# A fused attention and mixture-of-experts kernel: the weight roundings follow attention's older order, the last of them come behind it, and the last two rows go ahead of the first expert tile

## The reference

```python
def _L0_xattn_ref(hidden_states, memory_tokens, memory_mask):
    scores = einsum('bsd,bmd->bsm', hidden_states, memory_tokens) / sqrt(D)
    scores = where(memory_mask[:, None, :], scores, -1e30)
    readout = einsum('bsm,bmd->bsd', softmax(scores), memory_tokens)
    return where(any(memory_mask), readout, 0)

def _L0_ffn_ref(x, w_router, w_gate, w_up, w_down):   # 8 experts, 192 inner, top 2
    probs = softmax(xt @ w_router.T)
    top_v, top_i = top_k(probs, 2); top_v = top_v / sum(top_v)
    comb = zeros((T, 8)).at[arange(T)[:, None], top_i].add(top_v)
    g = einsum('th,eih->tei', xt, w_gate); u = einsum('th,eih->tei', xt, w_up)
    return einsum('tei,ehi,te->th', silu(g) * u, w_down, comb)

x = x + tanh(g_xattn[0]) * _L0_xattn_ref(_layernorm(x), ctx_2048, mask_BxS2_bk0)
x = x + tanh(g_ffn[0]) * _L0_ffn_ref(_layernorm(x), w_router, w_gate, w_up, w_down)
```

## Time and profile before

| | us |
|---|---|
| median of 3 runs (lowest, highest) | 289.17 (288.73, 289.31) |
| the profiled execution's own time | 288.54 |
| its span | 286.7 |
| PE busy / DVE busy | 250.5 / 176.5 |
| ACT busy / POOL busy | 149.9 / 165.7 |

### The profile page before, as it was taken

One profiled execution on the slowest core, in us unless ns is written; L12 is line 12 of the kernel. 1 busy time (PEld: TensorE's weight loads), 2 busy tenths in 40 slices (PEclk: granted clock), 3 DMA queues, 4 the chain that ended last, 5 costly groups with the idle time before them and its releaser, 6 DMA issues.

```text
span 286.7 us, 5375 instructions
## 1 busy us (share of the span) xinstructions
PE 250.5 (87%) x1464; PEld 210.7 (73%) x1464; DVE 176.5 (62%) x645; ACT 149.9 (52%) x308; POOL 165.7 (58%) x153
## 2 busy tenths in 40 slices
PE   0999888988797878779999999999999999999940
PEld 0876666765575556459999889999999999999920
DVE  4465497999999799486586644454444454444420
ACT  3477977767585663154353445445445445444430
POOL 1267786567476465063632565648778875777440
PEclk9999999999999999798999999999999999999995
DMA  6999999988988321255543467459888999588753
GB/s 210 386 394 336 325 303 341 328 261 287 288 274 264 133 110 39 74 169 167 114 75 41 74 119 177 80 93 163 171 168 155 154 169 173 98 157 157 126 73 40
DMA packets 25951, 52.08 MB, mean 182 GB/s; under 512 B 5249, under 2 KB 5377, under 8 KB 25921
## 3 DMA queue, kind: packets, MB, share of 16 engines
q0 software_dynamic: 8304, 19.83, 37.8%
q1 hardware_dynamic: 13008, 23.50, 25.1%
q10 hardware_dynamic: 4608, 8.39, 7.7%
HBM read 33.81 MB, written 17.89 MB: 180 GB/s over the span
## 4 chain that ended last, share of the span: by engine, by line
PE 46%; DVE 21%; DMA 9%; issue 9%; POOL 8%; ACT 4%; ACTq 1%; POOLq 0%; DVEq 0%
PE S L1305 6%; PE S L1309 6%; PE S L1306 6%; DMA out<-YT,IXE 5%; PE A L1295 4%; DVE st L698 4%; PE PO L1154 3%; DVE X L739 3%; PE PO L1326 2%; PE PO L1331 2%; PE PO L1330 2%; PE PO L1327 2%; PE PO L1328 2%; DVE TB L805 2%; POOL WGl L407 2%
## 5 line engine op out<-in xcount | busy, mean ns | idle before, releaser
L1305 PE MATMUL S<-WGh,XTh 128*128 x144 | 52.1, 362 | 0.1
L1306 PE MATMUL S<-WGl,XTh 128*128 x144 | 48.8, 339 | 0.0
L398 POOL TENSOR_TENSOR rs<-mv,CS 128x1 f32<-128x1 f32 x32 | 17.8, 556 | 46.4 <-DVE mv L704 45.8
L492 POOL DMA_INDIRECT out<-YT,IXI x19 | 30.1, 1585 | 15.1 <-issue 5.7
L589 ACT ACTIVATE SG<-S 128x192 f32<-128x192 f32 x36 | 11.9, 332 | 49.0 <-PE S L1309 43.2
L1030 DVE TENSOR_TENSOR H<-SG,S 128x192 f32<-128x192 f32 x36 | 12.7, 354 | 39.7 <-ACT SG L589 34.7
L424 POOL DMA_INDIRECT XG<-x2s,IXG x30 | 29.5, 985 | 9.6 <-issue 5.5
L1154 PE MATMUL PO<-CX,PT 128*128 128x512 f32 x64 | 32.8, 637 | 2.5 <-DVE X L739 1.9
L407 POOL TENSOR_TENSOR WGl<-WGl,WGh 128x512 fp32r<-128x512 f32 x24 | 30.3, 1273 | 5.8 <-ACT WGh L570 5.6
L1309 PE MATMUL S<-WGh,XTl 128*128 x144 | 31.0, 337 | 0.0
L1143 PE MATMUL S<-CT,XLT 128*128 128x256 f32 x128 | 30.9, 385 | 0.0
(11 more groups left out here) (168 smaller groups left out, 569.5 us busy)
## 6 DMA issues: line engine op xcount, KB each, us to landing
WGl<-in_wgu SPq DMA_DIRECT2D x24, 256.0 KB, 5.9
X<-in_x SPq DMA_DIRECT2D x16, 256.0 KB, 4.9
CT<-in_ctxt SPq DMA_DIRECT2D x8, 512.0 KB, 6.1
CX<-in_ctxn SPq DMA_DIRECT2D x8, 512.0 KB, 4.4
out<-X ACTq DMA_DIRECT2D x16, 256.0 KB, 4.9
x2s<-Y ACTq DMA_DIRECT2D x16, 256.0 KB, 3.9
WD1l<-in_wd SPq DMA_DIRECT2D x8, 256.0 KB, 5.4
WS<-in_wd SPq DMA_DIRECT2D x8, 256.0 KB, 5.3
```

The lines of the kernel that those rows point to most:

```text
L492: pool.indirect_dma_start(out=out, out_offset=bass.IndirectOffsetOnAxis(ap=to, axis=0), in_=yt(j), in_offset=None, compute_op=ALU.add)\
L1305: pe.matmul(o, XTh[:, j % 2, c, :], WGh[:, bass.ds(e, 1), c, :], start=(c == 0), stop=False)
L1306: pe.matmul(o, XTh[:, j % 2, c, :], WGl[:, bass.ds(e, 1), c, :], start=False, stop=False)
```

## The change

Five parts. (1) `SPLIT` has two units a step in steps 3 to 13, then 3, 4, 4, and the last 5 units are behind the loop (NA = 35). (2) The units have a new sequence, `UNITS`: experts 0 to 3 as before, then WD2 of experts 4 and 5, the rest of 4, WD2 of 6 and 7, the rest of 5, 6, 7. (3) In a step ACT rounds at the end; POOL takes the units of the step before, one ahead of each of its two `rstd`, and 11 units come behind gather(0). (4) Rows 14 and 15 go ahead of the first tile on ACT, DVE and PE: `weigh(5)` ahead of `xhi(0)`, `x2(15)` and its bias ahead of `xlo(0)`, `rt(13)` and `t2(14)` ahead of `gu(0)`. (5) PE's wait for all 40 units becomes, for tiles 0 to 4, a wait for the tile's own expert, and stands in full at tile 5.

```diff
-SPLIT = [0, 1, 2] + [3, 3, 2] * 4 + [3, 2]
-LATE = 5
+SPLIT = [0, 1, 1] + [2] * 11 + [3, 4, 4, 5]
+NA = sum(SPLIT[:NTK + 1])
+HEAD = 5
+UNITS = [(e, n) for e in range(4) for n in range(5)] + [(4, 4), (5, 4)] + [(4, n) for n in range(4)] \
+    + [(6, 4), (7, 4)] + [(e, n) for e in range(5, E) for n in range(4)]
...
@@ SP, loadw
-                if part(u)[1] == 4 and u >= 10:
-                    sp.wait_ge(s_wl, 5 * part(u)[0] - 5)
+                e, n = part(u)
+                if n == 4 and e >= 2:
+                    sp.wait_ge(s_wl, UNITS.index((e - 2, 4)) + 1)
...
@@ SP, step s: the store of comb now stands ahead of
                 for u in units(s + 2):
                     loadw(u)
@@ POOL, step s
-                if s <= LATE:
-                    for u in units(s - 1):
-                        lo(u)
+                for u in units(s - 1)[0:1]:
+                    lo(u)
                 if 0 <= s - 3:
                     rstd(mv2, s - 3, rs2, s_st2, s_rs2)
-                if s >= LATE:
-                    for u in units(s)[0:1]:
-                        lo(u)
+                for u in units(s - 1)[1:2 if s == NTK else NU]:
+                    lo(u)
                 if s + 2 < NTK:
                     rstd(mv1, s + 2, rs1, s_st1, s_rs1)
-                if s >= LATE:
-                    for u in units(s)[1:]:
-                        lo(u)
...
             gather(0)
+            for u in range(NA - 6, NA - 3):
+                lo(u)
             rstd(mv2, 14, rs2, s_st2, s_rs2)
...
             gather(2)
+            lo(NA - 3)
             rstd(mv2, 15, rs2, s_st2, s_rs2)
...
             gather(3)
-            pool.wait_ge(s_tne, 1)
-            early = pool.value_load(TNE[0:1, 0:1], min_val=0, max_val=(1 << 13) - 1)
+            for u in range(NA - 2, NA):
+                lo(u)
             stored(14, 15)
             for j in range(4, NX):
                 gather(j)
+            for u in range(NA, NU):
+                lo(u)
+            pool.wait_ge(s_tne, 1)
+            early = pool.value_load(TNE[0:1, 0:1], min_val=0, max_val=(1 << 13) - 1)
@@ ACT, yev: if j == 5, a wait for the POOL rounding of (7, 4)
@@ ACT, step s: the hi(u) of units(s) now stand behind exp(s - 1) in all steps
...
             evp(15)
-            xhi(0)
             weigh(5)
             act.activation(rsum[:, 0:1], rinv[:, 0:1], ACT.Silu)
+            for u in range(NA, NA + 2):
+                hi(u)
             store_x2(14)
             x2ln(14)
+            store_y2(14)
+            hi(NA + 2)
+            xhi(0)
+            ev2(14)
+            store_x2(15)
+            x2ln(15)
+            store_y2(15)
+            for u in range(NA + 3, NU):
+                hi(u)
...
@@ DVE
-            side += [coefs(5), top2(6), taken()]
-            weave(queue(x2(14), first_xlo(), nbias(mv2, rs2, nb2, 14, s_rs2, s_nb2), x2(15)), 2)
+            side += [coefs(5)]
+            weave(queue(x2(14), nbias(mv2, rs2, nb2, 14, s_rs2, s_nb2)), 2)
+            side += [top2(6), taken()]
+            weave(queue(x2(15), nbias(mv2, rs2, nb2, 15, s_rs2, s_nb2), first_xlo()), 2)
@@ PE
+            tp(15)
+            pe.wait_ge(s_ere, 1)
+            own, live = experts(0, ERE, 0), None
+            pv(15)
+            rt(13)
             pe.wait_ge(s_ixe, 1)
             pe.wait_ge(s_eje, 1)
             pe.wait_ge(s_inc, 1)
-            pe.wait_ge(s_ere, 1)
             tx(0)
-            rt(13)
-            own, live = experts(0, ERE, 0), None
-            pe.wait_ge(s_wl, NU)
+            t2(14)
             for j in range(NT):
                 with lives(pe, live, j):
+                    if j < HEAD:
+                        pe.wait_ge(s_wl, own[j] * 4 + 12)
+                    if j == HEAD:
+                        pe.wait_ge(s_wl, NU)
                     gu(j, own[j])
-                    if j == 0:
-                        t2(14)
-                    if j == 1:
-                        t2(15)
-                        rt(14)
                     if j + 1 < NT:
                         tx(j + 1)
                     if j == 0:
+                        t2(15)
+                        rt(14)
                         cum(5)
```

More of the change, by code:

```diff
@@ L283, in part @@
         def part(u):
-            return u // 5, (u % 5 if u < NU - 5 else (u - 1) % 5)
+            return UNITS[u]
         def wunit(u):
@@ L364, in _ @@
                     loadx(s + 3)
-                for u in units(s + 2):
-                    loadw(u)
                 if s >= 9 and s % 2 == 1 and (s - 9) // 2 < B:
@@ L371, in _ @@
                                  comb[:, 2 * b:2 * b + 2, :]).then_inc(s_scb[b >= EB], 16)
+                for u in units(s + 2):
+                    loadw(u)
             live = tiles_of(sp)
@@ L417, in odds @@
                     .then_inc(s_e2, 1)
+                last[0] = (s_e2, b + 1)
             def gather(j):
@@ L600, in yev @@
                 act.wait_ge(s_cj, j + 1)
+                if j == 5:
+                    act.wait_ge(s_wl, UNITS.index((7, 4)) + 1)
                 if j >= NB:
@@ L621, in _ @@
                     weigh((s - 7) // 2)
-                if s >= LATE:
-                    for u in units(s):
-                        hi(u)
                 if 0 <= s - 3 < NTK:
@@ L628, in _ @@
                     exp(s - 1)
-                if s < LATE:
-                    for u in units(s):
-                        hi(u)
+                for u in units(s):
+                    hi(u)
             ev2(13)
@@ L643, in _ @@
                 with lives(act, live, j):
-                    if j == 0:
-                        store_y2(14)
                     silu(j)
[L647 to L650, removed]
                     if j == AHEAD:
@@ L655, in _ @@
                     if j == 0:
-                        x2ln(15)
-                        store_y2(15)
+                        ev2(15)
                     if j >= 1:
@@ L1095, in _ @@
                     mul(j)
-                    if j == 0:
-                        for _ in nbias(mv2, rs2, nb2, 15, s_rs2, s_nb2):
-                            pass
                     if j == AHEAD:
@@ L1279, in _ @@
             t2(13)
-            tp(15)
-            pv(15)
             def experts(j, numbers, i):
```

## The result

After takes 299.3 us at the median (298.76 to 300.08, 4 runs), before in the same session 289.24 us (288.73 to 290.41, 4 runs): a ratio of 1.034, 95% interval 1.030 to 1.039, slower by 10.1 us. The forecast was 290.4 us with a range to 293.4, so it was wrong in size. The profiled execution took 298.76 us, with a span of 297.0.

What follows compares the result with a forecast made beforehand. No one engine bounds the whole: PE in the tiles, DVE in attention, neither early. Terms -2.5 - 3.8 + 7.2 + 0.3 = +1.2 on 288.54 gave 289.7, with 0.63 for the median 290.4 us; range 286.8 to 293.4.

Steps and rivals of the forecast that it cites:

- Fewer roundings in early steps: Steps 4 to 6: one rounding instead of three to five ahead of a `rstd`, ending DVE's waits; -2.5 us.
- no third rounding: Steps 8, 9, 10 and 13 lose one rounding each, so fewer 1.04 us meetings on DVE; -3.8 us.
- A load behind a wait: Step 12: X of row 14 queues on SP behind a weight load waiting for rounding 19, stopping DVE; +7.2 us.
- Rows 14 and 15 ahead, 11 roundings behind gather(0): Between attention and tiles, to out(1): earlier rows gain 1.8 us, late roundings hold DVE; net +0.3 us.
- Rival A: After gather(0): late roundings meet few DVE operations, so -1.8 in place of +0.3; 288.3 us, chance 22%.
- B: Step 12: X of row 14 lands late behind 768 KB of WS and CT, +2.6 us; 293.0 us, chance 15%.
- C: Step 12: DVE does not need that X, or SP gets past the wait; 281.8 us, chance 10%.
- D: Tiles: PE comes 1.5 us or more ahead of gather(10), idles, slow clock costs about 1.7; 292.1 us, chance 10%.
- PE's waits for weights: Tiles 0 to 5: units are done in time, including the wait for all 40 at tile 5; cost 0.

Runs made afterwards that it cites:

- the loads held back: After, with weight unit 21 and those behind it held on SyncE until the X loads of rows 14 and 15 are out: 289.6 us.
- the kernel with the roundings back: After, with before's unit order and numbers per step and all 40 roundings ahead of gather(0); rows 14 and 15 stay ahead: 287.1 us.
- the run with one wait ahead: After, with one GpSimd wait for tile 0's coefficient between gather(5) and the five last roundings, none between the five: 297.1 us.
- the run with the pauses: After, with two GpSimd waits among the five last roundings, for the coefficients of tiles 0 and 1: 295.13 us.
- the run with both waits ahead: After, with held loads, a wait for TB's last write ahead of roundings 29 to 31, and one for tile 0's coefficient ahead of the last five: 285.68 us.

## Why the prediction was wrong

*Fewer roundings in early steps, no third rounding* (-2.5 and -3.8): right in direction, and too small. Together they were to bring x2(9) to about 73; it came at 71.19. With the loads held back, x2(13) is 11.0 us ahead of before, 7.4 by x2(9) and 3.6 after it, where the two terms have 6.3.

*A load behind a wait* (+7.2): mechanism, place and step were right, and the step's growth came out at 7.26 us (15.22 against 7.96). Measured against the same kernel without the wait it is worth 9.7 us, and 10.5 us at x2(13) (107.70 against 97.2), because the steps would have been 6.0 us long there and not before's 8. The three terms together put x2(13) at +0.9; it came at -0.5. That it came so close is partly luck: the first two terms were 4.7 us too small and the third 3.3 us, with opposite signs.

*Rows 14 and 15 ahead, 11 roundings behind gather(0)* (+0.3, bounds -1.8 and +1.7): this step failed, both in its gain and in its cost. From x2(13) to out(1) after takes 9.1 us more than before. The term has two parts. The gain of 1.8 us by the order of the rows did not come: the kernel with the roundings back has that order and takes 38.0 us there, before 37.7. And the cost of the 11 roundings was 2.1 us (from -1.8 to +0.3), 1.7 for the three ahead of row 14 and what is left, 0.4, for the eight others, with no reason given but that they meet the side lists. Measured, the five last alone cost 7.9 us and the six others 6.4, each with the rest in place; the two overlap, since taking the six away lengthens the hold by the five. The prediction's own price, 1.04 us for each meeting, on all 11 would have given 11.4 us; its upper bound, +1.7, left room for three such meetings.

What the runs showed in its place is that nearly every late rounding keeps a DVE operation waiting for about its length, and that the side lists do not take that up: DVE is busy for 12.8 us more over the same 127 operations. With five single holds, as in rows 5, the five last still cost 5.7 us. On top comes a form that no row of before showed, one operation that stands for a whole series: ten of the 11 roundings stand in series of three, two and five, and 10 x 1.25 = 12.5 us is the bound for both forms. For the five last this second form is worth 2.2 us by the run with one wait ahead, and at most 4.2 by the run with the pauses.

*Rival A* (the late roundings fit, for 8.17 us of idle POOL) fell by the same; POOL's idle time said nothing, since the cost is on DVE. *B* did not happen in after: X was issued at 76.07 and used at 79.86, 3.8 us later. *C* is out by the 13.8 us wait of SP. *D*: the tiles from gather(10) on are not what moved; gather(10) comes 8.2 us late (173.67), as out(1) does by 8.6. *PE's waits for weights* at 0 was right for after, and wrong as soon as roundings stood among the tiles.

Of the 10.3 us between the spans, then: -7.0 by x2(9), +6.5 from there to x2(13), +9.1 to out(1), and 1.7 behind it (142.5 against 140.7 in the table). Those last 1.7 us have no cause that I could show; `rest` spreads over 140.0 to 142.7 between the kernels of the table.

## What to carry to other kernels

A GpSimd instruction put beside VectorE's critical chain is not free because GpSimd is idle there: charge VectorE about its length for each one, and more where it stands in a series directly behind a GpSimd DMA issue. What comes next in VectorE's queue decides what is late by it. A wait of GpSimd for VectorE's next result inside the series gave 4.2 us here and one ahead of it 2.2 us; check in the trace that the wait was not already met. And when loads are given a new order, look at each load with a wait for what stands behind it in its queue, two places down and not only one: here the X of two rows stood behind a buffer that came free a step too late, for 10 us.

## What the hardware showed

The length of a VectorE hold. Some operations get in when one rounding ends, also between two of a series: 1.24 and 1.22 us, 1.26 beside the 2.50 us pair above, 1.21, 1.17 and 1.19 in the run with both waits ahead, 1.28, 1.51 and about 1.30 three times in the run with one wait ahead. The short ones of these start 0.02 to 0.2 us behind the start of a rounding. Others stand until the last of the series is over: 3.20 us for two, 4.50 for three, 6.44 for five, 8.64 for seven. Nearly all of these start ahead of the first rounding, under a gather's or an output add's issue. Not all: the 8.64 us one starts at the same 120.54 as its rounding, and in the run with the loads of rows 14 and 15 first, whose timeline is

```profile
123.36 1.30 POOL L417 TENSOR_TENSOR WD1l<-WD1l,WD1h 128x512 fp32r<-128x512 f32 x1
123.41 6.17 DVE L1057 TENSOR_TENSOR cj<-XG,EJ 128x8 f32<-128x8 f32 x1
```
`cj` starts 0.05 us behind a rounding and stands for all five. So the start against the rounding does not decide. One thing is common to all whole-series holds in the traces, these two included: the first rounding begins within 0.03 us of the end of a GpSimd DMA issue, or under one, and the held operation begins under that issue or within 0.07 us of its end. Where GpSimd stood for 0.23 us or more between the issue and the first rounding (0.23 in the run with one wait ahead, 0.33 ahead of the three), or where no issue stood ahead, each operation waited for one rounding. The issue alone held nothing in before: its TB at 131.42 runs under a gather issued at 131.16, and three writes take 0.95 us. This is a pattern read from the traces; no run changed that gap alone, so why it decides stays open. That both forms happen, and that a wait of GpSimd for DVE ends the series, is shown.

The Trainium skill ("SBUF — State Buffer", section "SBUF: two separate sides") says that whichever of a GpSimd operation and a DVE operation with two SBUF inputs, or in a two-port mode, starts first has the shared port pair for the whole instruction, and that the other blocks fully. The single meetings agree with it (1.22 us beside 0.18). The 8.64 us beside seven instructions of about 1.25 us are more than one instruction; there the measurement decides.
